# Field-pair projection on one core: three buffers of x filled two tiles ahead, one turned copy of x filled in halves, TensorE's program written out

## What is computed

```
PAIRS = np.array(list(combinations(range(NUM_FIELDS), 2)), dtype=np.int32)
xi = x[:, pi, :]
xj = x[:, pj, :]
proj = jnp.einsum('bpd,pod->bpo', xi, W)
return proj * xj
```

## Time and profile before

| | |
|---|---|
| median of 3 runs | 676.4 us |
| the profiled execution's own time | 674.19 us |
| its span, first to last instruction | 672.4 us |
| TensorE, VectorE, GpSimd, ScalarE busy | 86%, 61%, 60%, 31% of the span |
| mean busy share of the 16 DMA engines | 9 tenths or more in all of the 40 slices but the first |
| moved | 285.20 MB, mean 424 GB/s |

### The profile page before, as it was taken

One profiled execution on the slowest core, in us unless ns is written; L12 is line 12 of the kernel. 1 busy time (PEld: TensorE's weight loads), 2 busy tenths in 40 slices (PEclk: granted clock), 3 DMA queues, 4 the chain that ended last, 5 costly groups with the idle time before them and its releaser, 6 DMA issues.

```text
span 672.4 us, 6957 instructions
## 1 busy us (share of the span) xinstructions
PE 578.1 (86%) x2704; PEld 346.3 (51%) x2704; DVE 412.5 (61%) x528; ACT 206.4 (31%) x257; POOL 404.4 (60%) x242
## 2 busy tenths in 40 slices
PE   5999897989898897889989889898989989889840
PEld 4565554646465464545636455464645546455420
DVE  1777485666666676566756656675666756656640
ACT  3333332333332232333323232242332323232210
POOL 1859467574766667476565756756566575756530
PEclk9999898998899899988979899898999989999775
DMA  8999999999999999999999999999999999999996
GB/s 339 394 430 438 442 414 448 428 426 434 433 426 439 422 448 418 443 420 437 426 421 436 424 442 429 434 426 425 431 436 424 428 418 436 435 427 431 438 427 293
DMA packets 12128, 285.20 MB, mean 424 GB/s; under 512 B 1680, under 2 KB 1808, under 8 KB 3536
## 3 DMA queue, kind: packets, MB, share of 16 engines
q1 hardware_dynamic: 9728, 270.28, 94.0%
q0 software_dynamic: 2016, 13.76, 4.9%
q10 hardware_dynamic: 368, 0.98, 0.4%
HBM read 25.89 MB, written 260.05 MB: 425 GB/s over the span
## 4 chain that ended last, share of the span: by engine, by line
DMA 56%; PE 27%; DVE 7%; POOL 5%; ACT 1%; issue 1%; SPq 0%; DVEq 0%; POOLq 0%
DMA out_dram<-staged 51%; PE proj L334 25%; DVE staged L384 7%; POOL staged L259 5%; DMA x_sb<-x_dram,rows_sb 3%; ACT staged L300 1%; DMA x_sb<-x_dram 1%; PE proj L312 1%; DMA ident_sb<-ident_dram 1%; PE proj L357 1%; ACT x_t L274 0%; POOL x_sb L242 0%; SPq L208 0%; DVEq L147 0%; POOLq L241 0%
## 5 line engine op out<-in xcount | busy, mean ns | idle before, releaser
L334 PE MATMUL proj<-w_sb,x_t 64*128 64x512 f32 (+7 forms) x2432 | 543.6, 551 | 54.6 <-DVE staged L384 53.2
L384 DVE TENSOR_TENSOR staged<-proj,x_sb 128x1024 f32<-128x1024 f32 (+7 forms) x528 | 412.5, 827 | 235.2 <-PE proj L334 161.9
L259 POOL TENSOR_TENSOR staged<-staged,x_sb 128x1024 f32<-128x1024 f32 (+4 forms) x224 | 389.7, 1754 | 201.3 <-ACT staged L300 198.6
L334 PEld LDWEIGHTS proj<-w_sb,x_t 64*128 64x128 f32 x2432 | 314.3, 194 | 280.5 <-issue 134.1
L300 ACT ACTIVATE staged<-proj 128x1024 f32<-128x1024 f32 (+4 forms) x224 | 174.0, 788 | 398.9 <-PE proj L334 304.6
L274 ACT ACTIVATE x_t<-proj 128x1024 f32<-128x1024 f32 x32 | 31.1, 1021 | 37.6 <-PE proj L312 37.6
L312 PE MATMUL proj<-ident_sb,x_sb 128*128 128x128 f32 x256 | 32.5, 282 | 7.4 <-DMA x_sb<-x_dram,rows_sb 7.3
L242 POOL DMA_INDIRECT x_sb<-x_dram,rows_sb x14 | 14.6, 1040 | 39.4 <-DVE staged L384 21.6
L312 PEld LDWEIGHTS proj<-ident_sb,x_sb 128*128 128x128 f32 x256 | 28.7, 144 | 13.0 <-DMA x_sb<-x_dram,rows_sb 11.4
L357 PE MATMUL proj<-ident_sb 128*128 128x128 f32 x16 | 3.6, 418 | 5.5 <-DMA ident_sb<-ident_dram 5.5
L357 PEld LDWEIGHTS proj<-ident_sb 128*128 128x128 f32 x16 | 3.3, 224 | 5.5 <-DMA ident_sb<-ident_dram 5.5
## 6 DMA issues: line engine op xcount, KB each, us to landing
out_dram<-staged SPq DMA_DIRECT2D x15, 5504.0 KB
out_dram<-staged SPq DMA_DIRECT2D x15, 5472.0 KB, 26.0
out_dram<-staged SPq DMA_DIRECT2D x15, 4896.0 KB, 26.7
out_dram<-staged SPq DMA_DIRECT2D x1, 3520.0 KB, 18.8
out_dram<-staged SPq DMA_DIRECT2D x1, 3008.0 KB
out_dram<-staged SPq DMA_DIRECT2D x1, 2784.0 KB, 22.6
out_dram<-staged SPq DMA_DIRECT2D x1, 2496.0 KB
out_dram<-staged SPq DMA_DIRECT2D x1, 2112.0 KB, 24.2
```

Of the source, the lines that this page charges most:

```text
L259: last = nc.gpsimd.tensor_tensor(product, product, x_sb[tile.parity][:, j * dim:(j + n) * dim], ALU.mult)
L334: last = nc.tensor.matmul(proj[b][h][:, at:at + width], x_t[tile.parity][half, i // 2, :], w_sb[half, col:col + width], start=True, stop=True)
L384: last = nc.vector.tensor_tensor(staged_part(item, i, j, n), proj[b][h][:, at:at + n * dim], x_sb[tile.parity][:, j * dim:(j + n) * dim], ...
```

## The change

x_sb gets a third buffer, and the load for tile t + 2 is issued during tile t. Its rows come by two gathers on GpSimd: first rows 16 to 19 (APART, load_apart, before step 3), which waits until tile t - 1 is done, then the other 124 (load_x, before step 10), which waits until the 4 rows have landed. ScalarE issues no loads of x any more. x_t has one buffer. It is filled in halves: the low 8 blocks of the next tile before step 16 (turn_low), when the steps left read only the high ones, and the high 8 blocks of this tile before step 8 (turn_high). A tile in the middle has 23 items now. With three buffers and 23 items a loop over two tiles doesn't fit, and TensorE's program is written out for all 16 tiles. The list of rows has twice the columns.

```
-SKIPPED = range(12, 20)
+APART = range(16, 20)
...
+    def tile_items(number):
+        for s in range(len(steps)):
+            if s == TURN_HIGH_BEFORE and number > 0:
+                yield "turn_high"
+            if s == TURN_LOW_BEFORE and number < tiles - 1:
+                yield "turn_low"
+            yield s
...
-        x_sb = [sb(f"x_sb{h}", [P, fields * dim]) for h in range(2)]
-        x_t = [sb(f"x_t{h}", [P, fields // 2, P]) for h in range(2)]
+        x_sb = [sb(f"x_sb{h}", [P, fields * dim]) for h in range(3)]
+        x_t = sb("x_t", [P, fields // 2, P])
...
+            def load_apart(number):
+                h, _ = loads_of(number)
+                if number >= len(x_sb):
+                    _, b, use = schedule[number - len(x_sb)][-1]
+                    pool.wait_ge(emptied[b][1], use + 1)
+                    pool.wait_ge(pool_scaled[group_of[pool_steps[-1]]], number - len(x_sb) + 1)
+                at = tiles + number
+                nc.gpsimd.indirect_dma_start(
+                    x_sb[h][APART.start:APART.stop, :], None, x,
+                    bass.IndirectOffsetOnAxis(ap=rows_sb[0:len(APART), at:at + 1], axis=0),
+                    bounds_check=batch - 1, oob_is_err=False).then_inc(x_apart_loaded[h], 16)
+            def load_x(number):
+                h, loads = loads_of(number)
+                pool.wait_ge(x_apart_loaded[h], 16 * loads)
+                nc.gpsimd.indirect_dma_start(
+                    x_sb[h][:], None, x,
+                    bass.IndirectOffsetOnAxis(ap=rows_sb[:, number:number + 1], axis=0),
+                    bounds_check=batch - 1, oob_is_err=False).then_inc(x_loaded[h], 16)
...
-            def load_skipped(tile):
...
-                act.dma_start(x_sb[1 - tile.parity][SKIPPED.start:SKIPPED.stop, :],
-                              x[row + SKIPPED.start:row + SKIPPED.stop, :]
-                              ).then_inc(x_rest_loaded[1 - tile.parity], 16)
...
-            each_tile(pe, emit)
+            every_tile(emit)
```

More of the change, by code:

```diff
@@ L75, with __init__ @@
 class Tile:
-    def __init__(self, number, parity, half, last=False):
-        self.number, self.parity, self.half, self.last = number, parity, half, last
-        self.first = isinstance(number, int) and number == 0
+    def __init__(self, number, tiles):
+        self.number, self.first, self.last = number, number == 0, number == tiles - 1
 def field_pair_project(nc, x, w, ident, rows, out, fields, dim):
@@ L86, in field_pair_project @@
     w_at, w_ends = w_columns(fields, dim)
-    assert 2 * dim == P and fields == 32 and tiles % 2 == 0 and tiles >= 4
+    assert 2 * dim == P and fields == 32 and tiles >= 4
+    assert all(i >= fields // 2 for s in range(TURN_LOW_BEFORE, len(steps)) for unit in steps[s] for i, _, _ in unit)
     assert all(2 * c == fields * dim for c in (UNIT,))
[L91 to L94, removed]
+    def tile_items(number):
[5 more added lines that the diff above has]
+            yield s
+    schedule, used = [], 1
+    for t in range(tiles):
+        here = list(tile_items(t))
+        schedule.append([(item, (used + n) % 2, (used + n) // 2) for n, item in enumerate(here)])
+        used += len(here)
     def items(tile):
-        for n, item in enumerate(last_tile if tile.last else whole_tile):
-            yield item, (1 + n) % 2, tile.number * per_tile + (1 + n) // 2
+        return schedule[tile.number]
     pool_steps = [s for s in range(len(steps) - 1) if s % 3 != 2]
@@ L136, in every_tile, with loads_of @@
         for t in range(tiles):
[L137 to L145, removed]
+            emit(Tile(t, tiles))
+    def loads_of(number):
+        return number % len(x_sb), (number + 1) // len(x_sb)
     with ExitStack() as ctx:
@@ L247, in emit @@
+            def load_x(number):
[5 more added lines that the diff above has]
+                    bounds_check=batch - 1, oob_is_err=False).then_inc(x_loaded[h], 16)
             def emit(tile):
                 for item, b, use in items(tile):
-                    if item == GATHER_BEFORE and not tile.first and not tile.last:
-                        if tile.number == 1:
+                    if item == APART_BEFORE and tile.number + 2 < tiles:
+                        if tile.first:
@@ L251, in emit @@
                             pool.wait_ge(rows_loaded, 16)
-                        load_x(tile)
+                        load_apart(tile.number + 2)
+                    if item == GATHER_BEFORE and tile.number + 2 < tiles:
+                        load_x(tile.number + 2)
                     if item not in pool_steps:
@@ L329, in project @@
                 for h in range(2):
-                    if not (tile.first and use == 0):
+                    if use:
                         pe.wait_ge(emptied[b][h], use)
@@ L334, in project @@
                         last = nc.tensor.matmul(
[L335 removed]
+                            proj[b][h][:, at:at + width], x_t[half, i // 2, :],
                             w_sb[half, col:col + width], start=True, stop=True)
@@ L372, in emit @@
                 for item, b, use in items(tile):
-                    if item == "turn":
+                    if item in LOW_PAIR:
                         continue
@@ L408 @@
         w[h * dim:(h + 1) * dim, :halves[h].shape[1]] = halves[h]
-    rows = np.arange(batch, dtype=np.uint32).reshape(-1, P).T.copy()
-    rows[SKIPPED.start:SKIPPED.stop] = NO_ROW
+    numbers = np.arange(batch, dtype=np.uint32).reshape(-1, P).T
+    rows = np.full((P, 2 * numbers.shape[1]), NO_ROW, np.uint32)
+    rows[:, :numbers.shape[1]] = numbers
+    rows[APART.start:APART.stop, :numbers.shape[1]] = NO_ROW
+    rows[:len(APART), numbers.shape[1]:] = numbers[APART.start:APART.stop]
     arrays = {
```

70 lines of the change are left out of this document (29 added, 41 removed).

## The result

The changed kernel takes 678.91 us (median of 16 runs, 676.81 to 681.1) against 676.4 us of the kernel before beside it (16 runs, 674.01 to 676.9): a ratio of 1.0045, 95% interval 1.0035 to 1.0054. By the ratio it is slower by 3.0 us, where I had forecast 1.9 us less, with a chance of 0.36 for faster and 0.41 for no change. The profiled execution took 679.12 us, with a span of 677.3 us, 4.9 us more than before. That is more than the 3.0 us, since the execution that was profiled before took 2.2 us less than the median.

The account below looks back on a forecast made before the run. The never-idle DMA engines, and the one that ends last, were taken as the bound. Its terms, -4.4 + 1.1 + 1.4 = -1.9 us from 676.4, gave 674.5 us, with a range of 672.3 to 679.0.

Parts of the forecast that it names:

- Three buffers, earlier loads: Waits of TensorE and GpSimd around gathers should go, worth 0 under VectorE's 5 us a tile of waits for stores.
- GpSimd ... : 0: A second gather instruction of 1.04 us, 14 times, costs 0, since GpSimd waits over 12 us a tile for ScalarE's copies.
- eat the 13 us of queued stores: A wait of some us for the 4 rows on GpSimd would first use up 13 us of stores already queued.
- ScalarE's rows away: Taking 14 loads of 8 rows off ScalarE's queue saves 4.4 us on the half of the DMA engines that ends last.
- fours: The 14 gathers of 4 rows move round the DMA engines, 3.5 rows each, adding 1.1 us.
- the shelf at a half: Sign in the tail: the DMA share's stay near a half, read as ScalarE's rows on eight engines, should disappear.
- The gather of 124 rows, the slow engine: Rival: rows 12 to 15 return to an engine spared for slowness; span 680 to 688, middle time 687 us; chance 0.17.
- even odds between the two: Whether the slow one of the two spared engines has rows 12 to 15 or 16 to 19 could not be read.
- The blocks: TensorE written out fetches some 15 more instruction blocks by DMA, adding 1.4 us on the last engine.
- Halves: Turning in halves makes ScalarE's two copies four, at worst 2.0 us a tile more on ScalarE, which has 7.0: 0.
- The middle share falls under 1.00 (then stores came late): Sign that would prove the forecast wrong: DMA engines no longer fully busy in the middle of the run.
- the fours on the same engines: Rival: gathers of 4 rows always hit the same four engines, +4.4 us there; no change, 676.9 to 677.8 us; chance 0.20.

Follow-up runs that it names:

- a1_rows_first: The changed kernel with the list of rows loaded third instead of last; 672.67 us, ratio 0.996 to the kernel before.
- a2_rows_wait: The kernel before with only GpSimd's wait for the list of rows moved into tile 0, before step 3; 679.92 us, ratio 1.0065.
- d1_act_eight: a1_rows_first with rows 12 to 19 loaded by ScalarE's queue two tiles ahead and 120 rows gathered; 675.09 us, ratio 0.9999 to the kernel before.
- b1_apart12: a1_rows_first with rows 12 to 15 apart instead of 16 to 19; 685.15 us, ratio 1.0139 to the kernel before.
- a4_fours: The kernel before, still two buffers and one tile of lead, with its loads replaced by GpSimd's gathers of 4 and 124 rows; 680.36 us, ratio 1.0075.
- c1_loop6: a1_rows_first with TensorE's tiles 2 to 13 in a loop of six tiles run twice; 672.99 us, ratio 0.9962 to the kernel before.

## Why the prediction was wrong

**The failed step** is the one on loads and queues: "Three buffers, earlier loads ... Worth 0", and with it "GpSimd ... : 0". I followed what the earlier loads need in a tile in the middle (a free buffer, the 4 rows) and what is queued behind these waits, but not what the first of them needs: the list of rows. My own piece of GpSimd's order of before shows rows_loaded on the gather of tile 1, and the piece after the change, also of tile 1, shows it no more. It had gone to tile 0, where it is not satisfied until 30.74 us. I had named what stands behind the wait for the 4 rows, and let it "eat the 13 us of queued stores" first. In the first slot of tile 0 there is no such queue of stores yet. The wait of 12.35 us held the second store back by 11.6 us (37.11 instead of 25.55) and left the DMA engines without work from about 35 to 37.5 us; and where they set the span, a us that they all miss is a us at the end.

**The size of it.** The two windows of the changed kernel, against a1_rows_first, miss (1.03 - 0.87 + 1.04 - 0.42) x 5 = 3.9 us. The spans differ by 5.9. The other 2 us are not idle time: the shares of the queues add up to 98.9% of 677.3 us = 669.8 us of busy time, and to 99.5% of 671.4 = 668.0 in a1_rows_first, for the same packets and bytes. These took some 2 us longer (with about 1 us of rounding), and why stays open. In a2_rows_wait, too, only 2.2 of the 4.4 us are missing work. That the wait is the cause of the whole difference is shown all the same, in both directions: a1_rows_first took 0.996 / 1.0045 = 0.9915 of the changed kernel's time, 5.7 us less, and a2_rows_wait 4.4 us more than the kernel before. The hole itself explains 3.9 of these 5.7 us.

**The sum of the rest.** Without the hole I had -1.9 us; a1_rows_first measured -2.7 (-3.7 to -1.8). By terms:

- The bound: the DMA engines, and the last of them. Right. The middle kept 1.00 and 430 GB/s, and the differences that the windows show lie at the start and in the tail.
- ScalarE's rows away -4.4, fours +1.1, together -3.3: measured -2.6 (a1_rows_first against d1_act_eight). The sign and nearly the size. That the size agrees so well is in part luck, since d1_act_eight has the eights without the step from which the 4.4 was read. The tail has neither the shelf at a half nor one at a quarter, which speaks for fours that move round. No view prints a packet's engine; but a packet begins as the one before it on its engine ends, and followed so in the trace of a1_rows_first, each gather of 4 falls on four engines that the gather before it did not use, and each engine gets 3 or 4 such rows in the run, as near as such following can tell; the forecast has 3.5. With the rule that the prediction cites of the Trainium skill, "DMA: Bandwidth & Descriptors", section on why a DMA increments its semaphore by 16 (a cursor that takes the engines in turn), the trace agrees.
- The gather of 124 rows, the slow engine: right that it is the great risk; it did not occur with rows 16 to 19 spared, and costs about 12 us with rows 12 to 15 spared. The even odds between the two were all that the trace of before gave.
- The blocks: 16 more, as worked out (about 15). Their +1.4 is not confirmed: by my terms d1_act_eight should be 1.4 us above the kernel before, and it is 0.1 below, interval -0.9 to +0.7. Either the blocks cost less or something else gave about 1 us back; no run separates them. Followed as above, the 21 blocks on q8 of a1_rows_first fall unevenly, none to three on an engine, where I had counted with none to two.
- Halves: ScalarE's 62 copies took 609 ns each (L298), so four cost 0.4 us a tile more than two of 1.02 us; VectorE kept its waits for stores. 0 as forecast.
- A second gather instruction, 0.97 us, and no wait for the 4 rows in the middle (L262 waited 0.2 us in 500). 0 as forecast there.
- q0: 2464 packets and not 2296. Small packets, of no weight in the sum.

**The signs that I had named.** q10, q8, the middle and the tail without a shelf came as foretold; the chain's stores in the middle took 23.5 to 24.9 us instead of about 26. "The middle share falls under 1.00 (then stores came late)" was the right sign for what happened, but I had tied it to the middle, and it stood at the start. The time of 678.9 us lies just inside the range, and that is luck: the case that made up this edge, the fours on the same engines, is not what happened. The case that decided, a wait for the list of rows in tile 0, was not among my rivals, though the order of GpSimd and the trace of before held all that it needed.

## What to carry to other kernels

When a transfer is issued earlier, list everything that its first issue waits for, also what is loaded only once (an index list, a constant), when that lands, and what is queued behind the wait on that engine in the first tile, where no backlog of stores covers it; read the trace's windows through the whole start, not from where it has become steady. In this kernel, bound by DMA, one load in the wrong place cost 5.7 us, and issuing it third, or putting the wait for it behind the first slot's work, turned 0.45% slower into 0.4% faster. The tail of the DMA share shows how evenly the 16 engines are loaded; count rows an engine, and know which partitions' engine is slow before rows are given back to it.

## What the runs showed of the hardware

- One DMA engine, that of partitions 16 to 19, is slower than the others: given back its share of 14 gathers, 56 rows of 8 KB that were worth 17.6 us at 0.314 us each, it ended the run alone and 12.2 us later (b1_apart12). So it does the same work in more time than the others.
- A gather of 4 rows among queued stores landed some 8.5 us after its instruction ended in the stretch shown (a4_fours); four store packets, as I had allowed it, are 6.4.
- Gathers of 4 rows fell on four engines each, in turn: 3 or 4 rows an engine after 14 of them (a1_rows_first).
- A list of rows issued at 8.99 us behind all other loads landed 21.75 us later (the changed kernel); what waits for it stands still so long.
- A loop with a body of six tiles fetched no fewer blocks of instructions than the program written out, 23 against 21 (c1_loop6, a1_rows_first), and TensorE stood still for 4.17 us at the branch back.
